# A selective scan with 16 sequences on one core: spread tensors by way of DRAM, a longer work ring, and side work placed anew

## The reference

```python
xr = x @ W_in.T + b_in;  xi, res = split(xr, 2)              # 512 features each
xi = silu(causal_conv(xi, W_conv, taps=4) + b_conv)
proj = xi @ W_x.T + b_x
delta = softplus(proj[..., :512]); B, C = proj[..., 512:528], proj[..., 528:]
dA = exp(delta[..., None] * -exp(A_log)); dBx = delta[..., None] * B * xi[..., None]
h[t] = dA[t] * h[t-1] + dBx[t]                               # 512 features x 16 states
y = sum_n(h * C) + xi * D;  y = (y * silu(res)) @ W_out.T + b_out
x = layernorm(x + y)
gf = sigmoid(net3(mean over t of x));  out = x
for _ in range(3):
    tf = sigmoid(w4(gelu(w3(gelu(w2(gelu(w1(out))))))))
    out = out + (0.1 + range * (0.7 * gf + 0.3 * tf - 0.5) * 2) * twist(out)
return layernorm(x + out)
```

## Time and profile before

| | |
|---|---|
| time, median of 3 runs | 4628.59 us (4626.33 to 4634.05) |
| the profiled execution's own time | 4633.1 us |
| its span, first to last instruction | 4631.3 us |
| mean granted TensorE clock | 0.873 of full speed |
| bytes moved by DMA | 529.62 MB, mean 114 GB/s |

### The profile page before, as it was taken

How to read it: one execution, slowest core, us unless ns; L and a number is a source line. 1 busy time by engine, 2 the same in 40 slices (tenths; PEclk the granted TensorE clock), 3 DMA queues, 4 the chain that set the end, 5 groups by cost and what they waited for, 6 DMA issues and landing times.

```text
span 4631.3 us, 53910 instructions
## 1 busy us (share of the span) xinstructions
PE 3639.7 (79%) x18112; PEld 1619.7 (35%) x18112; DVE 3565.9 (77%) x2784; ACT 3059.8 (66%) x3936; POOL 3648.9 (79%) x1602
## 2 busy tenths in 40 slices
PE   6668878788787877878688787887978788786765
PEld 2223343343333433343243433433333343433323
DVE  0887878888787887877788787887888788788871
ACT  2545857678585776858668485775858668585753
POOL 2987979889687887978879687887878879787871
PEclk8778988889898897988889898898988889898877
DMA  4454454634545444444634545445444634545430
GB/s 133 101 132 100 107 137 98 163 83 117 132 101 135 110 122 115 107 126 99 160 83 121 129 103 144 99 117 128 98 127 111 149 91 120 133 104 134 101 77 27
DMA packets 305603, 529.62 MB, mean 114 GB/s; under 512 B 77616, under 2 KB 210736, under 8 KB 305072
## 3 DMA queue, kind: packets, MB, share of 16 engines
q1 hardware_dynamic: 305328, 526.18, 46.4%
HBM read 154.67 MB, written 69.21 MB: 48 GB/s over the span
## 4 chain that ended last, share of the span: by engine, by line
ACT 26%; PE 25%; POOL 16%; SPq 11%; DVE 10%; issue 8%; DMA 3%; DVEq 0%; POOLq 0%; ACTq 0%
ACT L657 10%; POOL work L944 9%; ACT da L721 7%; PE banks L513 5%; DVE da L870 4%; POOL work L951 3%; PE banks L519 3%; SPq L371 3%; ACT big L692 3%; PE banks L504 3%; SPq L344 3%; DVE work L870 3%; SPq L338 3%; PE banks L593 3%; PE y_sum L635 3%
## 5 line engine op out<-in xcount | busy, mean ns | idle before, releaser
L944 POOL TENSOR_TENSOR work<-u_q,b_quad 128x1024 f32<-128x1024 f32 x1024 | 2394.6, 2359 | 424.6 <-DMA b_quad<-bc_scratch 194.8
L870 DVE TENSOR_TENSOR_SCAN da<-da,work 128x1024 f32<-128x1024 f32 x640 | 1465.4, 2290 | 355.8 <-ACT da L721 256.6
L721 ACT ACTIVATE da<-delta_q,neg_a 128x1024 f32<-128x1024 f32 x1024 | 1129.9, 1113 | 676.0 <-DVE work L878 572.5
L951 POOL TENSOR_TENSOR work<-work,c_quad 128x1024 f32<-128x1024 f32 x384 | 904.7, 2356 | 244.2 <-DVE work L870 242.3
L635 PE MATMUL y_sum<-work,v_all 128*32 128x256 f32 x8192 | 663.6, 430 | 417.2 <-DVE work L878 260.6
L878 DVE TENSOR_TENSOR work<-da,c_quad 128x1024 f32<-128x1024 f32 x640 | 782.4, 1223 | 211.7 <-DMA c_quad<-bc_scratch 191.0
L870 DVE TENSOR_TENSOR_SCAN work<-da,work 128x1024 f32<-128x1024 f32 x384 | 875.6, 2280 | 48.8 <-ACT da L721 48.3
L657 ACT ACT_TABLE_LOAD x575 | 737.7, 1283 | 35.9 <-DVE neg_mean L853 17.2
L635 PEld LDWEIGHTS y_sum<-work,v_all 128*32 128x32 f32 x8192 | 217.5, 116 | 894.3 <-DVE work L878 352.1
L526 PE MATMUL banks<-xi,w_all 128*128 128x512 f32 x1024 | 490.2, 629 | 15.7 <-ACT soft L816 12.7
L513 PE MATMUL banks<-xi,taps 128*128 128x512 f32 (+3 forms) x1024 | 458.1, 598 | 12.5 <-DVE big L895 11.7
(11 more groups left out here) (71 smaller groups left out, 3542.3 us busy)
## 6 DMA issues: line engine op xcount, KB each, us to landing
delta_q<-delta SPq DMA_DIRECT2D x1024, 128.0 KB, 2.4
u_q<-u SPq DMA_DIRECT2D x1024, 128.0 KB, 2.5
res_scratch<-s_std SPq DMA_DIRECT2D x64, 512.0 KB, 3.3
s_quad<-res_scratch SPq DMA_DIRECT2D x1024, 32.0 KB, 1.9
b_quad<-bc_scratch SPq DMA_DIRECT2D x256, 128.0 KB, 3.0
c_quad<-bc_scratch SPq DMA_DIRECT2D x256, 128.0 KB, 3.9
yg<-s_quad SPq DMA_DIRECT2D x1024, 32.0 KB, 1.9
x_feat<-in_xT SPq DMA_DIRECT2D x16, 1024.0 KB, 5.5
```

The source lines that it names most:

```text
L721: act.activation(da[:, t % 2, :], delta_q[:, slot, :], ACT.Exp, scale=neg_a[:, t % PERIOD:t % PERIOD + 1]).then_inc(da_ready, 1)
L870: dve.tensor_tensor_scan(dst, da[:, t % 2, :], work[:, slot, :], 0.0, ALU.mult, ALU.add) \
L944: pool.tensor_tensor(work[:, slot, :], u_q[:, copied, :], b_quad[:, j, :], ALU.mult) \
L951: pool.tensor_tensor(work[:, un % WORK, :], work[:, un % WORK, :], c_quad[:, un % PHASE, :], ALU.mult) \
```

## The change

- **Delta and u**: each is stored to DRAM once per block (`store_delta`, `store_u`), and delta_q and u_q are filled from there, 128 rows per transfer, with a source that repeats 32 rows four times. u is written into the buffer `soft`.
- **B and C**: one transfer per 128 rows; its source is four rows, each 32 times. bc_scratch is stored with one transfer.
- **Gated rows**: s_quad holds two slots of two phases. One gate serves two phases (y_sum uses both halves of its bank). Rows go to y_scratch in DRAM (`store_y`) and come back in quarters of a sequence (`load_yg`), each of which releases one task of the output projection.
- **Ring** `work`: 7 slots; REDUCE_LAG 2: TensorE reduces GpSimd's products one step later.
- **Norm**: ScalarE keeps logarithm and exponential; VectorE subtracts the mean and scales, straight from PSUM. neg_mean and shift are gone.
- **Places**: tables of steps for side work and for SP's transfers are new; two functions of one table stand together more often.

SP issues 303 transfers per batch before and 96 after; ScalarE loads 575 tables before and 485 after.

```diff
-WORK = 5
+WORK = 7
-REDUCE_LAG = 1
+REDUCE_LAG = 2
...
-            def copy_quads(g):
+            def store_delta(m):
+
+                sp.wait_ge(delta_ready, 2 * m + 2)
+                if m >= 2:
+                    for g in range(QUAD * (m - 2), QUAD * (m - 1)):
+                        sp.wait_ge(dq_in[g % COPIES], 16 * (g // COPIES + 1))
+                sp.dma_start(d_dram[m % 2], delta[:, :]).then_inc(d_stored, 16)
...
+            def load_delta(g):
 
                 c, slot, m = g % QUAD, g % COPIES, g // QUAD
-                sp.wait_ge(delta_ready, 2 * m + 2)
-                if (before := g - COPIES) >= 0:
-                    sp.wait_ge(da_ready, PHASE * before + PHASE)
-                for n in range(QUAD):
-                    sp.dma_start(delta_q[GROUP * n:GROUP * n + GROUP, slot, :],
-                                 delta[GROUP * c:GROUP * c + GROUP, :]).then_inc(dq_in[slot], 16)
...
+                sp.wait_ge(d_stored, 16 * (m + 1))
+                if g >= COPIES:
+                    sp.wait_ge(da_ready, PHASE * (g - COPIES) + PHASE)
+                sp.dma_start(delta_q[:, slot, :], d_dram[m % 2, GROUP * c:GROUP * c + GROUP, :].unsqueeze(0)
+                             .broadcast_to([QUAD, GROUP, SEQ])).then_inc(dq_in[slot], 16)
...
-                for k in range(QUAD):
-                    sp.dma_start(s_quad[GROUP * k:GROUP * k + GROUP, c, :],
-                                 res_dram[b % 2, m, GROUP * c:GROUP * c + GROUP, QT * k:QT * k + QT]) \
-                      .then_inc(sq_in[c], 16)
...
+                for i in range(2):
+                    sp.dma_start(s_quad[:, slot, i, :],
+                                 res_dram[b % 2, m, GROUP * (c + i):GROUP * (c + i + 1), :]
+                                 .rearrange("p (k t) -> k p t", k=QUAD)).then_inc(sq_in[slot], 16)
...
+                for i in range(2):
+                    sp.dma_start(y_dram[b % 2, m, GROUP * (c + i):GROUP * (c + i + 1), :]
+                                 .rearrange("p (k t) -> k p t", k=QUAD),
+                                 s_quad[:, slot, i, :]).then_inc(y_stored[slot], 16)
...
+                sp.dma_start(yg[:, n % 2, :, :],
+                             y_dram[f % 2, :, :, QT * n:QT * n + QT].rearrange("m p t -> p m t")).then_inc(yg_in[n % 2], 16)
...
-                for n in range(QUAD):
-                    sp.dma_start(tile[GROUP * n:GROUP * n + GROUP, j, :],
-                                 bc_dram[first + QUAD * j + n:first + QUAD * j + n + 1, :].partition_broadcast(GROUP)) \
-                      .then_inc(signal[j], 16)
+                sp.dma_start(tile[:, j, :], bc_dram[first + QUAD * j:first + QUAD * j + QUAD, :].unsqueeze(1)
+                             .broadcast_to([QUAD, GROUP, SEQ])).then_inc(signal[j], 16)
...
-                for r in range(2):
-                    a = act.activation(dst[:, r, :], banks[:, bank, r * DM:(r + 1) * DM], ACT.Identity,
-                                       bias=shift[:, i, r:r + 1], scale=r_std[:, i, r:r + 1])
-                a.then_inc(norm, 1)
...
-                dve.tensor_scalar(neg_mean[:, i, :], mean_var[:, i, :, 0], -1.0, 0.0, ALU.mult, ALU.add).then_inc(neg, 1)
...
+                dve.wait_ge(rstd, n + 1)
+                for r in range(2):
+                    ins = dve.tensor_scalar(dst[:, r, :], banks[:, bank, r * DM:(r + 1) * DM], mean_var[:, i, r, 0:1],
+                                            r_std[:, i, r:r + 1], ALU.subtract, ALU.mult)
+                ins.then_inc(norm, 1)
...
-                dve.wait_ge(sq_in[c], 64 * (g // QUAD + 1))
-                dve.tensor_tensor(s_quad[:, c, :], y_sum[:, 0:QT], s_quad[:, c, :], ALU.mult).then_inc(gated, 1)
+            def gate(pair):
+
+                slot = pair % 2
+                dve.wait_ge(reduced, phase_reduced(2 * pair + 1))
+                dve.wait_ge(sq_in[slot], 32 * (pair // 2 + 1))
+                dve.tensor_tensor(s_quad[:, slot, :, :], y_sum[:, :].rearrange("p (i t) -> p i t", i=2),
+                                  s_quad[:, slot, :, :], ALU.mult).then_inc(gated, 1)
```

More of the change, by code:

```diff
@@ L128, in cycle_position, with batch_at, block_at @@
     return CYCLE_AT[c] + F_AT[i]
[L131 to L138, removed]
+def batch_at(t, position):
+    f, rest = divmod(t - position, PERIOD)
+    return f if rest == 0 and 0 <= f < BATCH else None
+def block_at(t, table):
+    for ahead in range(3):
+        m = t // (4 * PHASE) + 1 - ahead
+        if 0 <= m < BATCH * DC and t == 4 * PHASE * (m - 1) + table[(m - 1) % DC]:
+            return m
+    return None
 def side_tasks(t):
@@ new lines, in store_y @@
+            def store_y(pair):
+                b, m, c, slot = pair // 8, (pair // 2) % DC, 2 * (pair % 2), pair % 2
+                sp.wait_ge(gated, pair + 1)
+                if b >= 2 and pair % 8 == 0:
+                    for i in range(2):
+                        sp.wait_ge(yg_in[i], 32 * (b - 1))
+                for i in range(2):
+                    sp.dma_start(y_dram[b % 2, m, GROUP * (c + i):GROUP * (c + i + 1), :]
+                                 .rearrange("p (k t) -> k p t", k=QUAD),
+                                 s_quad[:, slot, i, :]).then_inc(y_stored[slot], 16)
@@ new lines, in _ @@
+                for c in range(QUAD):
+                    if (m := block_at(t, (DLD_AT[c],) * DC)) is not None:
+                        load_delta(QUAD * m + c)
+                    if (m := block_at(t, (ULD_AT[c],) * DC)) is not None:
+                        load_u(QUAD * m + c)
+                if (t - YST) % (2 * PHASE) == 0 and 1 <= (t - YST) // (2 * PHASE) <= 8 * BATCH:
+                    store_y((t - YST) // (2 * PHASE) - 1)
+                for n in range(4):
+                    if (f := batch_at(t - PERIOD, YGLD_AT[n])) is not None:
+                        load_yg(f, n)
@@ L435, in _ @@
+                for h in range(2):
+                    if (f := batch_at(t - PERIOD, OUT_AT[h])) is not None:
+                        sp.wait_ge(e_norm, 4 * f + 2 * h + 2)
+                        sp.dma_start(out[f, h * L:(h + 1) * L, :].rearrange("(k p) c -> p k c", p=P),
+                                     x1[:, 4 * h:4 * h + 4, :]).then_inc(out_done[h], 16)
+                if (f := batch_at(t, XRES_AT)) is not None:
                     if f:
@@ L463, in _ @@
+                for j in range(PHASE):
+                    if (nb := batch_at(ahead, LB_AT[j])) is not None:
+                        load_b(nb, j)
+                    if (nb := batch_at(ahead, LC_AT[j])) is not None:
+                        load_c(nb, j)
             for h in range(2):
@@ L547, in couple @@
                         for k in range(4):
[L548 removed]
+                            pe.matmul(half, yg[:, n % 2, k, r * P:r * P + P], w_out[:, k, :], start=k == 0, stop=False)
                         pe.matmul(half, eye, b_out, start=False, stop=False)
```

294 lines of the change are left out of this document (134 added, 160 removed).

## The result

The changed kernel takes **5797.8 us** (5791.5 to 5803.7) against 4627.7 before: ratio 1.2525 [1.2503, 1.2547]. The forecast was 5340 with a range of 4850 to 5850, slower.

A forecast was written before the change was run, and what follows sets the result against it. No engine is full; interruptions of the scan loop, mainly transfers at batch boundaries, were taken to count. Then 93 + 20 us ahead, 15 batches of 321 (4815), a last of 268 and 142 behind: 5338, forecast 5340 us, range 4850 to 5850.

The forecast's parts named there:

- Four engines: Transfers with 4 outermost use only four of sixteen engines: 5.1 us per 512 KB load, 300 us a batch on each.
- rival 2: Four engines, all waits inside their queue, so only the queue's own time is left: 4720 to 4850 us; chance 0.06.
- rival 3: Four slower engines at 13.8 GB/s each: 495 us a batch, 8200 us in all; chance 0.04.
- batch without any wait: A batch with no transfer wait: 60 units in 234 us, 3.9 each, 250 us in all.
- boundary (units 60-67): From delta of unit 60 to product of unit 67: thirteen 5.1 us loads, 74 us with others, against 31: +43 a batch.
- gated rows: Return through DRAM delays the output projection 19 us; four units of cover leave 10 us a batch (0 to 15).
- inside (units 15, 31, 47): Delta and u stored, then reloaded: 17 us against 15.6; stall of about 6 us (0 to 12), three times a batch: 18.
- −240: Whole-run gain from all but the transfers: ScalarE −120, gate −80, its own time with VectorE's exchange −10, ring −30.
- ScalarE: Norm and 90 table loads taken off it, 307 us less work, 0.39 of its time on the path: −120 us.
- Gate: One gate per two phases: half of VectorE's 161.0 us wait for TensorE, −80 us; own time 105.2 to about 90.
- Ring: Longer work ring and REDUCE_LAG 2: a fifth of GpSimd's 141.9 us wait for a slot, −30 us (0 to −142).
- Rival 1: All sixteen engines serve every transfer: −240, −170 on c_quad, +50 for the detour, 4273 us, faster; chance 0.08.

The follow-up runs named there:

- Experiment 2: Changed kernel with partitions ordered feature-major, so delta, u, B and C loads have 32 outermost instead of 4: 4347.2 us, ratio 0.9392 to before the change.
- experiment 5: Against the 4347.2 us feature-major kernel: s_quad loads and y stores as four issues each, 4294.9 us; output projections later, 4267.5; both together, 4215.7.

## Why the prediction was right, and where its size was off

**Four engines: right.** 10,608 small packets were forecast as about 10,600. The load of 5.1 us is 4.80 in SP's rhythm. 0.33 of DMA share is 0.309. Waits over 1000 us are 1625. Rivals 2 and 3 are out: rival 2 ended at 4850 us, and an engine at the 13.8 GB/s of rival 3 would need 9.5 us a load. Units 0 to 3 took 50.3 us ("over 50"). Experiment 2 settles it: without loads on four engines the kernel is 6% faster than before, not 25% slower.

**Ends of the loop: right.** The first scan was forecast at 113 and came at 112.5 us; behind the last lie 142 us, as forecast. The whole error is in the batch: 351.1 us instead of 321, and 15 × 30 = 450 of the 458. (The first batch takes 301 us and the last 318, because each boundary falls on two batches; the sum is the same.)

**The range: partly luck.** Its high end stood on 350 us a batch, and 351.1 is just over that. The time stays inside because the sixteen batches come to 5535 us, with a shorter first and last one, and the high end counted 16 × 350 = 5600.

**The steps of the 321.** Measured are the intervals of the scans, against experiment 2, whose loads use sixteen engines, and against before for unit 7:

```
                           forecast   measured   from
batch without any wait       250        253.5    259.6 in experiment 2, less 6.1 in unit 7 (10.8, before 4.7)
boundary (units 60-67)       +43        +53.3    87.0 - 33.7
gated rows                   +10        +13.9    unit 7: 18.5 - 4.7
inside (units 15, 31, 47)    +18        +23.3    7.9 + 7.8 + 7.7
other units                    0         +7.1    units 50-52 4.8, 19 and 23 3.4, less elsewhere
sum                          321        351.1
```

- *Boundary: mis-sized.* The mechanism is as forecast: the four engines work almost without a gap (of the stretches between 1431 and 1520 us only two, 8 us in all, are under 0.25, at 0.19). Stretches of the changed kernel in which nearly every other engine stands still (columns as in the earlier trace rows):

```profile
1455.00:1460.00 5.00, 0.00 (x0) 0.00 (x0) 0.00 (x0) 0.00 (x0) 0.00 (x0) 0.50 0.25 89
1460.00:1465.40 5.40, 0.00 (x0) 0.00 (x0) 0.00 (x0) 2.15 (x2) 0.00 (x0) 0.50 0.26 105
```

  0.25 is four of sixteen. Thirteen loads, 4.9 us from start to start, are 64 us of the 87, close to the 66 forecast. The term that was too small is what stands between them: the forecast's 74 left 8 us for it, and the trace has 23. Ahead of the last load of C SP's queue holds four transfers of s_quad and y_scratch, the stores of delta, u and out, and the 1 MB of x_res. By the forecast's own prices that is 4 × 1.6, and 3 × 1.6 and 3.3 at 20 GB/s an engine, 14 to 15 us and not 8. What the other 8 or 9 are stays open.
- *Gated rows and inside a batch: mis-sized,* both within their bounds (0 to 15, 0 to 12 a block). A store and a load behind it were priced at 3.3 us to landing for the store; on the busy queue delta_scratch takes 5.7 by the page (4.0 in experiment 2). The stall of "about 6 us" does not follow from its own terms either: 17 + 2.4 − 15.6 is 4, so the forecast was nearer to the 7.8 than its terms were. And the 7.8 come on top of intervals of 7.2 and 6.0 us that units 15 and 31 still have in experiment 2.
- *The base: right in sum.* With all of experiment 5 a batch takes 250.5 us. Its parts were less right, as follows.

**The parts of −240.** *ScalarE:* −120 forecast, up to 94 + 77 = 171 measured by taking back, in two different kernels; ScalarE's time is worth more than its share of the chain over its share of busy time (0.39): 94 of 180 us busy in the norm, 77 of 117 in the table loads, 0.5 to 0.7. *VectorE's new operation:* 533 ns instead of 411, so 20 us more busy time; its longest takes 545 ns and the longest of the moments beside it 433, while the longest neg_mean before took 4361. The Trainium skill ("SBUF — State Buffer", who interferes with whom, and "VectorE: DVE Perf Modes", why PSUM operands drop a tier) had led to this: it lets a tensor_scalar take the port pair shared with GpSimd with operands in SBUF, but not with one in PSUM. The trace agrees; no run puts the same operation in both places. *Gate:* its wait for TensorE falls from 161.0 to 30.5 us and its own time from 105.2 to 86.4, more than the half that was forecast; what that is worth in the span was not isolated. *Ring:* −12 measured of −30.

**Rival 1** (4273, sixteen engines) is what experiments 2 and 5 tried: 4347, and 4267 with the output projections two units later. Its 170 us on c_quad were right (191.0 to 24.4). Its 50 us for the detour look short: moving the readers alone gives back 80, though not all of that need be the detour's.

## What to carry to other kernels

Count issues, but look at the shape of each before you merge them: the dimension that stands first in the pattern sets how many engines carry it (up to sixteen), and the same copy with its broadcast inside instead of outside was worth 1450 us here. Read the DMA share per engine that can take part: 0.31 was a full queue. When a tensor takes a detour through DRAM, move the work that reads it as well (up to 80 us here), and keep operations that share a table in one place (77 us).

## What the runs showed of the hardware

- A DMA issue is not a fixed cost: 0.5 us with little ahead of it, 4.80 us behind a row of loads dealt to four engines, 10.79 us for two issues together. Transfers for all sixteen wait behind them: a store to res_scratch lands after 11.7 us, against 5.9 in experiment 2 and 3.3 before.
- With one load of 512 KB in flight, time does not scale with engines: 12.8, 9.3, 6.7 and 4.6 us for 2, 4, 8 and 16.
- TensorE's granted clock follows the stalls: 0.84 in units 4 to 63 of the changed kernel, 0.93 in experiment 2, and 0.50 (1.2 GHz) in the stretches above in which it did nothing.
